# Attention kernel: both half weighings of a pair issued together at every fourth step, output copies behind exponentials 3 and 35

## What is computed

```python
scores = jnp.einsum('bshd,bthd->bhst', q, k) * (1.0 / np.sqrt(DK).astype(np.float32))
a = jax.nn.softmax(scores, axis=-1)
o = jnp.einsum('bhst,bthd->bshd', a, v).reshape(b, s, DH)
```

## Time and profile before

| what | us |
|---|---|
| median of three runs | 1828.25 |
| lowest and highest | 1827.03, 1828.65 |
| the profiled execution | 1830.83 |
| its span, first to last instruction | 1828.7 |
| its mean granted TensorE clock (share of 2.4 GHz) | 0.975 |

### The profile page before, as it was taken

One profiled execution on the slowest core, in us unless ns is written; L12 is line 12 of the kernel. 1 busy time (PEld: TensorE's weight loads), 2 busy tenths in 40 slices (PEclk: granted clock), 3 DMA queues, 4 the chain that ended last, 5 costly groups with the idle time before them and its releaser, 6 DMA issues.

```text
span 1828.7 us, 40066 instructions
## 1 busy us (share of the span) xinstructions
PE 1709.0 (93%) x15395; PEld 666.2 (36%) x15396; DVE 1607.1 (88%) x2290; ACT 1476.8 (81%) x2809; POOL 653.2 (36%) x932
## 2 busy tenths in 40 slices
PE   6799999999999999999999999999999799799784
PEld 4332222222222222278722222222222245466553
DVE  7799999999999999945499999999997587499777
ACT  6569999999999999943389999999999667767455
POOL 1423310132444444200035565556600133133447
PEclk9899999999999999999999999999999999899897
DMA  4422122211121111278511211121102343422121
GB/s 125 167 70 90 55 88 65 65 57 34 61 67 58 56 57 62 67 205 226 162 48 51 65 51 49 51 63 54 39 12 55 91 131 99 134 67 55 40 71 46
DMA packets 151358, 142.15 MB, mean 78 GB/s; under 512 B 38987, under 2 KB 130126, under 8 KB 151011
## 3 DMA queue, kind: packets, MB, share of 16 engines
q1 hardware_dynamic: 142818, 122.36, 22.6%
q0 software_dynamic: 8352, 17.29, 3.4%
HBM read 76.60 MB, written 60.03 MB: 75 GB/s over the span
## 4 chain that ended last, share of the span: by engine, by line
PE 75%; DVE 9%; ACT 9%; issue 3%; DMA 2%; POOL 1%; SPq 0%; POOLq 0%; DVEq 0%; ACTq 0%
PE PS L1971 29%; PE PS L2068 18%; PE PS L1955 10%; ACT probs L1317 7%; PE PS L2018 4%; PE PS L2003 2%; PE PS L2112 1%; PE PS L2118 1%; PE PS L2181 1%; DVE hst L1089 1%; PE PS L1995 1%; DVE VP L1066 1%; DVE VP L1074 1%; PE PS L2324 1%; DVE MXV L1095 1%
## 5 line engine op out<-in xcount | busy, mean ns | idle before, releaser
L897 DVE TENSOR_REDUCE mxp<-PS 128x1 f32<-128x1024 f32 x1024 | 1171.7, 1213 | 33.9 <-PE PS L1955 29.2
L1317 ACT ACTIVATE probs<-PS 128x512 f32<-128x512 f32 x2048 | 1095.9, 597 | 71.4 <-PE PS L2068 28.2
L1971 PE MATMUL PS<-probs,VH 128*32 128x256 f32 x8192 | 643.1, 391 | 2.3 <-ACT probs L1317 1.0
L2068 PE MATMUL PS<-stacks 51*128 51x512 bf16 x2048 | 442.9, 387 | 22.8 <-ACT probs L1317 18.6
L1955 PE MATMUL PS<-stacks 48*128 48x512 bf16 x2048 | 417.7, 380 | 10.0 <-DMA stacks<-qkl_d 8.8
L1971 PEld LDWEIGHTS PS<-probs,VH 128*32 128x32 f32 x8192 | 173.1, 108 | 401.6 <-issue 223.7
L2068 PEld LDWEIGHTS PS<-stacks 51*128 51x128 bf16 x2048 | 116.1, 93 | 463.4 <-ACT probs L1317 378.9
L1664 POOL DMA_INDIRECT S<-oe_d,ROWI x128 | 130.2, 1017 | 133.5 <-PE PS L1971 126.8
L1634 POOL DMA_INDIRECT xe_d<-S,ROWI x128 | 125.1, 977 | 140.1 <-PE PS L1971 117.8
L1612 POOL CAST spl<-nmx 128x8 bf16<-128x8 f32 x64 | 12.7, 199 | 305.4 <-DVE nmx L853 227.2
L1955 PEld LDWEIGHTS PS<-stacks 48*128 48x128 bf16 x2048 | 105.2, 95 | 34.7 <-DVE mxp L897 13.6
(11 more groups left out here) (361 smaller groups left out, 1849.8 us busy)
## 6 DMA issues: line engine op xcount, KB each, us to landing
stacks<-qkl_d SPq DMA_DIRECT2D x128, 96.0 KB
xe_d<-zt SPq DMA_DIRECT2D x16, 640.0 KB
XNT<-xe_d SPq DMA_DIRECT2D x32, 320.0 KB, 3.8
oe_d<-XNT SPq DMA_DIRECT2D x32, 320.0 KB, 3.2
stacks<-qkl_d SPq DMA_DIRECT2D x128, 64.0 KB
o_d<-SG SPq DMA_DIRECT2D x256, 32.0 KB
ews<-in_ew_dram SPq DMA_DIRECT2D x33, 192.0 KB, 2.4
stacks<-qkl_d SPq DMA_DIRECT2D x128, 32.0 KB
```

What stands on the lines that cost most here:

```text
L897: v.tensor_reduce(mxp[:, n // 2, n % 2:n % 2 + 1], MXB[n % 2].rearrange("p a c -> p (a c)"), X_AX, ALU.max).then_inc(mx_done, 1)
L1317: act.activation(probs[:, at:at + 512], PS[:, bank_of(u, e), :], ACT.Exp, scale=float(1.0 / np.sqrt(np.float32(DK)))).then_inc(exp_done, 1)
L1971: mm = pe.matmul(OB[32 * jg:32 * jg + 32, c:c + 256], VH[w][:, kt, :], probs[:, at:at + 256], start=(kt < 2 and half == 0), stop=(kt >= TC ...
L2068: pe.matmul(PS[:, bank_of(u, e), :], KS[w][o:o + KROWS + 3, kt * P:(kt + 1) * P], QS[w][o:o + KROWS + 3, q0:q0 + 512], start=True, stop=Tr ...
```

## The change

Two edits. On TensorE both halves of a pair are issued together, at each step e with e % 4 == 3, directly after that step's score and ahead of that step's maximum products; steps 4k+1 have no weighing, and the exceptions at 5, 7, 37 and 39 go. The wait for the unit's values moves from after the products of step 1 to directly after the score of step 3. On ScalarE the copies of outputs follow exponentials 3 and 35 instead of 4 and 36. The same matmuls, exponentials and copies are issued as before, in the same number.

```diff
--- before.py
+++ after.py
@@ -1316,9 +1316,9 @@
                     at = (6 * (w % 2) + e) % RING * 512
                     act.activation(probs[:, at:at + 512], PS[:, bank_of(u, e), :], ACT.Exp,
                                    scale=float(1.0 / np.sqrt(np.float32(DK)))).then_inc(exp_done, 1)
-                    if e == 4 and u > 0 and u != EXPERTS_AT:
+                    if e == 3 and u > 0 and u != EXPERTS_AT:
                         evac(u - 1, 0, 1)
-                    if e == 36:
+                    if e == 35:
                         evac(u, 0, 0)
                     if u == RANK_UNIT and e == RANK_EXP:
                         act.wait_ge(lg_ready, 3)
@@ -2067,6 +2067,14 @@
                     o, kt, q0 = 64 * (e % 2), e // 2 % TCH, e // 2 // TCH * 1024 + e % 2 * 512
                     pe.matmul(PS[:, bank_of(u, e), :], KS[w][o:o + KROWS + 3, kt * P:(kt + 1) * P], QS[w][o:o + KROWS + 3, q0:q0 + 512],
                               start=True, stop=True).then_inc(sc_ready, 1)
+                    if e == 3:
+                        pe.wait_ge(vh_ready, u + 1)
+                    if e % 4 == 3:
+                        wu, pair = divmod(weighed // 2, TCH)
+                        if EXPS * wu + 4 * pair + 4 <= EXPS * u + e:
+                            weigh(wu, pair, wu % 4, 0)
+                            weigh(wu, pair, wu % 4, 1)
+                            weighed += 2
                     if u == RANK_UNIT and e == RANK_EXP:
                         ranks()
                     elif u == RANK_UNIT and e == RANK_EXP + 1:
@@ -2074,13 +2082,6 @@
                     elif chunk < min(CHUNKS * UNITS, CHUNKS * (u + 1) + AHEAD + CHUNKS * (e + 1) // EXPS):
                         max_chunk(chunk)
                         chunk += 1
-                    if e == 1:
-                        pe.wait_ge(vh_ready, u + 1)
-                    for turns in range({5: 0, 7: 2}.get(e % (EXPS // 2), e % 2)):
-                        wu, pair = divmod(weighed // 2, TCH)
-                        if EXPS * wu + 4 * pair + 4 <= EXPS * u + e:
-                            weigh(wu, pair, wu % 4, weighed % 2)
-                            weighed += 1
                     if u == UNITS - 1 and e == 19:
                         pe.wait_ge(mx_done, CHUNKS * UNITS)
                         residual_sum(0)
```

## The result

The changed kernel takes **2013.91 us**, the median of four runs (2013.83 to 2015.48), against 1827.64 us for the kernel before beside it. The ratio is 1.1021 with a 95% interval of 1.1002 to 1.104: 186 us slower. The forecast was 2016 us, slower, in a range of 1988 to 2047.

What follows compares the result with a forecast made beforehand. Before, TensorE's sequence, VectorE's pace and the bank loop bound within 5%; after, the loop at 2.68 us a block. Units +191, less 3 us of stalls, gave +188 on 1828.25: 2016 us, range 1988 to 2047.

Steps and rivals of the forecast that it cites:

- three limits: Kernel before: TensorE's sequence 2.24 us a block, VectorE's pace 1.13 us a maximum, the bank loop 1.07 or 1.14 us.
- the bank loop: Score e waits for exponential e-3 to free its bank; claimed to pace changed blocks at 2.68 us, chance 0.86.
- The links of the loop: From score 4k+3 to score 4k+7: 0.32 + 1.00 + 0.22 + 0.49 + 0.65 = 2.68 us.
- VectorE doesn't stretch it: VectorE's maxima, with products 0.45 and then 2.23 us apart, add 0 to 0.05 us per block.
- The copies cost nothing where they are: ScalarE's copies behind exponentials 3 and 35 fall into its new gap: 0, at most 0.1 us twice a unit.
- TensorE saves its switches: One pair instead of two halves saves switches into and out of weighing matmuls: 0.14 us per block, sequence 2.24 to 2.10.
- The sum: Unit 42.74 against 36.73 us, +6.01; thirty units 180, units 0 and 18 together 11, less 3: +188 us.
- Stray stalls of before: Stalls in single units of the stage before the change; 3 us of them were let vanish in the slack.
- The first unit: Unit 0 of the stage, with nothing to weigh at step 3: given +5.4 us.
- The last unit: Most blocks lack maximum products (2.46 us), but residual products lie in the loop in full; left at +6.0 us.
- the one after the experts: Unit 18, with nothing to weigh at step 3: given +5.4 us.
- The clock as a rival: TensorE idles and its clock falls: blocks at double time 4.2 us, a tenth of them +79: 2095 us, chance 0.05.

Runs made afterwards that it cites:

- The table of banks: Four runs with half of the maximum work left out: old order 1831.9 us with three banks, 1834.9 with four; changed order 1931.9 and 1737.9.
- the run with the product on the lower rows: Changed kernel, three banks, half of the maximum products and maxima left out, keeping those on the lower rows instead of the upper: 2454.42 us, ratio 1.3426.

## Why the prediction was right, point by point

- *What bounds the kernel.* That three limits lay within 5% in the kernel before, and that one of them, the bank loop, shows in no busy share, was the step on which all else stood. The table of banks shows the bank loop: the old order doesn't need the fourth bank, the new one does. VectorE was within 5% too, but did not set the pace (an undisturbed unit takes 36.73 us with and without half of its work).
- *The links of the loop.* Score to pair 460.19 - 459.87 = 0.32; pair to products 461.19 - 460.19 = 1.00, the one link that no row of before showed; products to score 0.23; score to exponential 461.89 - 461.42 = 0.47 (0.49 taken); exponential to score 0.65. Sum 2.67 for 2.68.
- *VectorE doesn't stretch it.* Right: 0.03% with its work nearly halved.
- *The copies cost nothing where they are.* Right. Timeline of a pair, the copy, and the next exponential:

```profile
454.96 1.07 PE L1971 MATMUL PS<-probs,VH 128*32 128x256 f32 x16
...
456.10 0.60 ACT L1306 ACTIVATE SG<-PS 128x512 f32<-128x512 f32 x1
...
456.60 2.06 ACT L1317 ACTIVATE probs<-PS 128x512 f32<-128x512 f32 x4
```

  The copy starts 456.10 - 454.96 = 1.14 after the pair began, as in the earlier trace rows, and exponential 4 follows at 456.60, when its score (456.19) allows it. Behind exponentials 4 and 36 they would have cost 15 us.
- *TensorE saves its switches.* The saving is real: a pair costs 1.00 where two halves cost 1.14. It is hidden behind the loop, and comes out with four banks, where a block is 1.98 us in one order and 2.22 in the other (a unit 32.59 and 36.42). Only 0.14 of these 0.24 us is the saving; the other 0.10 goes with scores that run beside products in the new order, which no run shows by itself. That changing the tiling mode drains TensorE, as the Trainium skill says in TensorEngine Tiling (Array Packing), Key Properties, agrees with the 0.14 us, though no run tells a drain from another cost of the switch. By that rule alone the sign would have been wrong here.
- *The sum.* A unit +5.93 for +6.01. The stage grew by 182 us for 188. Stray stalls of before: I let 3 us vanish, but the 28 ordinary units took 37.09 us each on the mean before where an undisturbed one is 36.73, and 42.73 after where it is 42.66, so of 10 us of stray stalls 8 vanished. The first unit: I gave it 5.4, and it went from 39.1 to 46.1 us, since the clock was lower for more of it (mean 0.74 in the first 20 us of the stage, 0.91 before). The last unit grew by 5.1 for 6.0, the one after the experts by 5.5 for 5.4. Outside the stage came 4.6 - 3.3 = 1.3 us that are not the change's, and the medians lie 186 us apart where the two profiled executions lie 183. So the block and the unit were forecast rightly; that the time came within 2 us of 2016 is luck, the sum of errors of up to 5 us with both signs. (The upper end of the range, 2016 and 32, is 2048 and not 2047.)
- *The clock as a rival.* It did not come in the changed kernel, apart from these few microseconds. Its price, 4.2 us for a block at double time, is what the run with the product on the lower rows showed where it did come: a unit of 67 us is 16 blocks of 4.2. I had argued against it from a stretch with scores and weighings; a kernel with less product work and the same order fell to it. So 0.05 was not too much for it.
- *What would show it.* Waits of scores for exponentials were forecast as 130 to 170 us in some 500 places (158.7 in 501), ScalarE's near 300 (278), VectorE's near 200 (172).

## What to carry to other kernels

Before two pieces of work of an in-order queue are put together, follow each ring of buffers round once: producer's start, consumer's start, release, and everything that the queue has between the producer's last and next item. If that sum is near the pace, a longer uninterrupted piece inside it lengthens every trip, even though the engine that does it gets faster: here a piece of 1.00 us instead of 0.57 made a block of 2.24 us one of 2.67. A buffer more turns the same edit into a gain (with half of the maximum work left out, 1932 to 1738 us, against 1835 for the old order with that buffer). Look for such a loop where several engines are over 90% busy and no one is plainly last.

## What the runs showed of the hardware

- The granted clock can stay at half for hundreds of microseconds while the engine's row is solidly busy. With the product of a chunk on the upper rows left out the changed order of work ran 355 and 887 us at a stretch at 0.50 (1.2 GHz) with TensorE busy 66.87 of 67.04 us in a unit; with the one on the lower rows left out instead, at the same number of instructions, it ran at 1.00 nearly throughout (1932 us). The old order with the lower product left out and three banks also ran at 0.50 for 68 us at the start of the stage in its profiled execution. In the slow kernel the clock rose at 465 us, right after four products on all 128 rows. Which property of the work decides between the two I didn't settle.
- A product on the upper rows and a score on the lower rows run beside each other, also across the two kinds of work: their rows start less than 0.01 us apart (501.54 and 501.55), and the exponential comes 0.51 us after the score's row. On the same half the row of the score starts just as early, but its exponential comes 0.70 us after it (block 2.67 and not 2.49). So of matmuls that share rows, the start in the trace isn't the start of their work; the consumer tells.
